# Softmax reciprocals of an attention kernel: two of 256 columns in place of four of 128

## The reference

```python
qkv = X @ W_qkv + b_qkv                     # 16 heads, 64 each for Q, K, V
scores = einsum('bhqd,bhkd->bhqk', Q, K) / sqrt(64)
attn = softmax(scores, axis=-1)             # over 1024 keys
out = einsum('bhqk,bhkv->bhqv', attn, V)
return out @ W_fc + b_fc
```

## Time and profile before

| | us |
|---|---|
| median of 3 runs | 1827.69 |
| lowest and highest | 1825.25, 1830.28 |
| the profiled execution | 1822.86 |
| its span in the trace | 1821.4 |
| busy in the span: TensorE | 1644.4 (90%) |
| VectorE | 1345.1 (74%) |
| POOL | 1130.2 (62%) |
| ScalarE | 829.1 (46%) |

### The profile page before, as it was taken

The page is one execution under the profiler, slowest core; times in us unless marked ns, Lnnn a source line. Parts: engine busy times, 40 slices in busy tenths (PEclk is TensorE's granted clock), DMA queues, the critical chain, the costliest instruction groups (busy, mean ns, idle before and its releaser), DMA issues. The chain is left out here.

```text
span 1821.4 us, 29000 instructions
## 1 busy us (share of the span) xinstructions
PE 1644.4 (90%) x9675; PEld 900.1 (49%) x9675; DVE 1345.1 (74%) x2143; ACT 829.1 (46%) x1144; POOL 1130.2 (62%) x519
## 2 busy tenths in 40 slices
PE   4789999999999999999999999999999999945996
PEld 3444444444444444444444444444445444434886
DVE  5678777777777777777777777777777777587887
ACT  3344444444444444444444444444444444325874
POOL 3366766776766667667676666766776766720134
PEclk8899999999999999999999999999999999968999
DMA  2000000000000000000000000000000001000010
GB/s 87 18 18 18 18 18 17 17 17 17 17 17 17 17 17 1 16 17 17 17 17 17 17 17 17 17 17 17 17 17 17 17 13 49 1 24 24 30 36 29
DMA packets 31040, 37.07 MB, mean 20 GB/s; under 512 B 2174, under 2 KB 25243, under 8 KB 31003
## 3 DMA queue, kind: packets, MB, share of 16 engines
q1 hardware_dynamic: 30848, 36.58, 6.2%
q10 hardware_dynamic: 154, 0.03, 0.0%
HBM read 14.58 MB, written 2.10 MB: 9 GB/s over the span
## 5 line engine op out<-in xcount | busy, mean ns | idle before, releaser
L511 POOL TENSOR_TENSOR ACC<-ACC,PR 128x1024 f32<-128x1024 f32 x382 | 908.4, 2378 | 345.4 <-ACT PR L548 325.8
L548 ACT ACTIVATE PR<-ps_s 128x1024 f32<-128x1024 f32 x512 | 501.1, 1024 | 525.9 <-PE ps_s L754 504.7
L586 DVE TENSOR_REDUCE NMH<-ps_mx 128x2 f32<-128x1024 f32 x507 | 617.6, 1218 | 151.7 <-PE ps_mx L734 148.4
L764 PE MATMUL ps_o<-PR,V 128*64 128x512 f32 x2048 | 507.6, 614 | 4.4 <-ACT PR L548 1.1
L734 PE MATMUL ps_mx<-KHI,QHI 64*128 64x512 f32 x1014 | 234.5, 457 | 60.0 <-DVE NMH L586 60.0
L622 DVE RECIPROCAL SUM<-SUM 128x128 f32<-128x128 f32 x256 | 240.4, 941 | 6.4 <-ACT SUM L539 6.4
L764 PEld LDWEIGHTS ps_o<-PR,V 128*64 128x64 f32 x2048 | 106.1, 135 | 272.4 <-ACT PR L548 252.6
L511 POOL TENSOR_TENSOR ACC<-PR 128x1024 f32<-128x1024 f32 x64 | 150.8, 2356 | 143.0 <-ACT PR L548 143.0
L748 PE MATMUL ps_s<-QHI,KHI 64*128 64x512 f32 x1024 | 210.6, 406 | 17.6 <-DVE QLO L600 16.3
L734 PEld LDWEIGHTS ps_mx<-KHI,QHI 64*128 64x128 f32 x1014 | 95.4, 184 | 255.3 <-DVE NMH L586 161.1
L750 PE MATMUL ps_s<-QLO,KHI 64*128 64x512 f32 x1024 | 203.9, 391 | 0.0
(11 more groups left out here) (192 smaller groups left out, 1722.2 us busy)
## 6 DMA issues: line engine op xcount, KB each, us to landing
hcur<-hT SPq DMA_DIRECT2D x32, 512.0 KB, 3.3
Wraw<-in_L_attn_W_qkv SPq DMA_DIRECT2D x32, 192.0 KB, 3.0
x<-in_L_attn_X SPq DMA_DIRECT2D x4, 512.0 KB, 5.2
Wfc<-in_L_attn_W_fc SPq DMA_DIRECT2D x32, 64.0 KB, 2.5
hT<-in_L_attn_X SPq DMA_DIRECT2D x4, 512.0 KB, 6.3
out<-e_res SPq DMA_DIRECT2D x7, 256.0 KB, 2.3
e_hTs<-hT_hi SPq DMA_DIRECT2D x6, 256.0 KB, 2.3
e_hTs<-hT_lo SPq DMA_DIRECT2D x6, 256.0 KB, 2.4
```

Of the source, the lines that this page charges most:

```text
L511: G.tensor_tensor(ACC[:, ch, :, :], a, PR[:, t, :, :], ALU.add).then_inc(added, 1)
L548: A.activation(PR[:, t, :, :], ps_s[:, i:i + 2, :], ACT.Exp, scale=SCALE).then_inc(exp_done, 1)
L586: D.tensor_reduce(NMH[:, ch, i, kc, :], banks, AX, ALU.max, negate=True).then_inc(mx_red, 1)
L764: last = T.matmul(ps_o[half(h), ch, :], V[:, u, t, half(h)], PR[:, t, h, :], start=(t == 0), stop=(t == 7))
```

## The change

The table INVERT loses its entries at (1,0), (2,0), (5,0) and (6,0); those at (1,1), (2,1), (5,1) and (6,1) now name parts 0 and 1. A part is 256 columns instead of 128, and O waits for two counts per chunk in place of four. In `last` two parts stand in place of four. Nothing else differs, and the result is computed from the same numbers.

```diff
--- before.py
+++ after.py
@@ -398,8 +398,8 @@
         SUMS = {0: (-1, 1), 4: (0, 0)}
         SUMS_BANK = 3
 
-        INVERT = {(1, 0): (-1, 1, 0), (1, 1): (-1, 1, 1), (2, 0): (-1, 1, 2), (2, 1): (-1, 1, 3), (3, 0): (-1, 1, "O"),
-                  (5, 0): (0, 0, 0), (5, 1): (0, 0, 1), (6, 0): (0, 0, 2), (6, 1): (0, 0, 3), (7, 0): (0, 0, "O")}
+        INVERT = {(1, 1): (-1, 1, 0), (2, 1): (-1, 1, 1), (3, 0): (-1, 1, "O"),
+                  (5, 1): (0, 0, 0), (6, 1): (0, 0, 1), (7, 0): (0, 0, "O")}
         LAST_ON_POOL = 6
         FIRST_UNITS = (("k", 0, ps_s[:, 0, :]), ("k", 1, ps_s[:, 1, :]), ("q", 0, ps_s[:, 2, :]), ("q", 1, ps_s[:, 3, :]),
                        ("v", 0, ps_o[:, 0, :]), ("v", 1, ps_o[:, 1, :]))
@@ -613,11 +613,11 @@
             def invert(m, ch, part):
 
                 if part == "O":
-                    dve.wait_ge(recip, 4 * (2 * m + ch + 1))
+                    dve.wait_ge(recip, 2 * (2 * m + ch + 1))
                     wait(dve, fc_mm, 2 * m + ch)
                     D.tensor_tensor(O[:, :], ps_o[:, ch, :], SUM[:, :], ALU.mult).then_inc(o_norm, 1)
                 else:
-                    q = slice(part * P, part * P + P)
+                    q = slice(part * 256, part * 256 + 256)
                     dve.wait_ge(sums_in, 2 * m + ch + 1)
                     D.reciprocal(SUM[:, q], SUM[:, q]).then_inc(recip, 1)
 
@@ -676,7 +676,7 @@
                     dve.wait_ge(added, 7 * (2 * NP - 1) + t - 1)
                     D.tensor_tensor(ACC[:, 1, :, :], ACC[:, 1, :, :], PR[:, t, :, :], ALU.add).then_inc(added, 1)
                 unit("fc", NP - 1, 1, 0, ps_s[:, 0, :])
-                for part in (0, 1, 2, 3, "O"):
+                for part in (0, 1, "O"):
                     invert(NP - 1, 1, part)
                 unit("fc", NP - 1, 1, 1, ps_s[:, 1, :])
```

## The result

The changed kernel takes 1836.1 us (median of 20 executions, 1828.6 to 1838.8) against 1828.4 us (20, 1825.3 to 1831.0) before: a ratio of 1.0038, 95% interval 1.0029 to 1.0047. It is slower by 7 us by the ratio (7.7 on the medians), a little beyond the 0.3% that a measurement of this kernel can tell. The profiled execution has a span of 1834.5 us against 1821.4. That is 13.1 us, more than the medians differ by, since the profiled execution of the kernel before took 1822.86 us, less than any of those 20.

The account below looks back on a forecast made before the run. TensorE was taken to set the pace, VectorE mattering only where TensorE waits for it. A 3.1 us stall less 0.06 at the end gave +3.0 us, 1830.7 us on the median's scale, range 1825 to 1839.5.

Parts of the forecast that it names:

- The wide reciprocal: A reciprocal of 256 columns on VectorE: 1.73 us, against 0.941 us for the narrow one of 128.
- Place (2,1): Behind block 2's second reduce: the wide reciprocal delays block 3's first reduce, stalling TensorE 0.10 us in 31 pairs, 3.1 us.
- Place (6,1): Behind block 6's second reduce: block 7's first reduce ends late, a 0.04 us stall that the V matmuls take back; cost 0.
- Places (1,1) and (5,1): Behind the second reduces of blocks 1 and 5, before the projections: 0.78 us more fits VectorE's 1.5 us idle; cost 0.
- The sum: Whole kernel: 3.1 us of stall in 31 pairs less 0.06 at the end, together +3.0 us.
- The range: Whole kernel: from 1825 us (all hidden, less the lowest run's 2.4 us) to 1839.5 us (a wide reciprocal of 1.88 us).
- the likeliest case: The small stall of TensorE before block 3's first reduce: 1830.7 us, +0.17%.
- the case to which I gave 0.30: Whole kernel slower by more than 0.3% (5.5 us), by any cause; chance 0.30.
- a wide one that saves nothing: Rival before block 3's first reduce: a wide reciprocal takes 1.88 us, total 1839.5 us; chance 0.30 with all other losses.
- What would show it: Signs in the profile: 1.73 us reciprocals, about 31 more maxima matmul waits, VectorE busy time down some 10 to 20 us.
- At the end: Behind the last chunk: two wide reciprocals take 3.33 us in place of 3.39 for four narrow ones, a gain of 0.06.

Follow-up runs that it names:

- p192_320: The changed kernel with its 512 columns cut into 192 and 320 in place of 256 and 256: 1859.6 us, 1.0161 against the kernel before.
- wide_ch0: The changed kernel with wide reciprocals only for chunk 0 and four narrow ones for chunk 1: 1828.5 us, 0.9997 against the kernel before.

## Why the prediction was right, and where it fell short

- *The wide reciprocal*: 1.73 us forecast, 1.742 measured.
- *Place (2,1)*: the reduce of (3,0) was to start 2.78 us behind that of (2,1) and does, at 2.80 (619.77 to 622.57). A stall of 0.16 less 0.06 from the V matmuls, so 0.10; the pair grew by 0.08, and the V matmuls went from 2.00 to 1.94 as forecast. The step holds, and p192_320 shows its slope.
- *Place (6,1)*: cost 0, as forecast (wide_ch0: 47.79 us). There the V matmuls took 1.96 us.
- *Places (1,1) and (5,1)*: "cost 0" holds in the regular pairs, where idle time of 0.7 us is left ahead of L600. It failed in the second pair. The step that failed is that I looked at one regular pair and took it for all: I named gate_rows in the description and never followed what stands behind the reciprocal there. Price 2.9 us, once.
- *The clock* was missing from the sum. By the profiles, stretches at 1.2 GHz in the loop cost 1.5 us each.
- *The sum*: +3.0 us forecast, +7.7 measured on the medians of the two kernels, +6.9 by the ratio. 2.4 stall and 2.9 waits make 5.3, so 1.6 to 2.4 us remain. The clock was my candidate for them, since the profiles of kernels with the stall at (2,1) have 3, 2, 1, 3, 1 and 4 stretches in the loop and those without it 0, 0, 1, 1 and 1. That is one execution each. The record has the mean granted clock of every execution, and by it the clock's part is smaller: 80 executions of the kernel before (those for which it stands) average 0.9725 and 1828.8 us, 25 of the changed one 0.9718 and 1835.4 us, and within either kernel 0.001 less clock goes with 0.9 to 1.1 us more. Of the 6.5 us between the averages the clock then makes 0.7, and 5.8 stay at an equal clock, near the 5.3 of the two waits. The three stretches against none, 4.5 us, are a difference between two single executions, of which the one before took 1822.86 us at a mean clock of 0.978. Nor is the part behind the attention still: with the same code it took from 220.2 to 229.1 us over these profiles.
- *The range* held the time (1825.0 to 1839.5), and the mechanism of the likeliest case acts near the size forecast (2.4 us for 3.1), but the change went over 0.3% and so into the case to which I gave 0.30. The range reached that far up for the price of a wide one that saves nothing. That rival did not act; the second pair took its place, and that the time stayed in the range is luck in that part.
- *What would show it*: I expected the new wait in the idle time of the maxima matmuls. It was in that of their weight loads, 161.1 to 178.6 us, 186 to 247 times. VectorE's busy time fell by 8.8 us, a little less than the 10 to 20 that I gave. At the end the reciprocals took 3.37 us in place of 3.39 (3.33 forecast).

## What to carry to other kernels

In an in-order queue that another engine waits on, the length of each single instruction counts, not the number: two long ones in place of four short ones save 8.8 us of busy time and cost 2.4 us where one stands in front of a reduce with 0.25 us of slack, and nothing where idle time of 1.5 us follows. Follow every unrolled pair of a loop, not the regular one alone. And before shaving a queue that is 74% busy, look at the one long wait for it: moving one instruction by one place there gave 62 us.

## What the runs showed of the hardware

- A reciprocal costs 6.2 ns a column and 0.15 us more, from 4 to 320 columns (171, 353, 941, 1343, 1742, 2141 ns for 4, 32, 128, 192, 256 and 320; each within 10 ns of that).
- The steps of gate_rows (512 columns on VectorE) last from 0.52 to 2.8 us, and those followed here by the point of POOL's add at which they start; the split of 256 columns lasts 0.43 us ahead of the adds and 2.2 us, at most 2.6, beside them. The reciprocals never do (1694 to 1753 ns over 128 of them).
- Each stretch at 1.2 GHz in a regular pair of 47.8 to 47.9 us (at 226, 994, 464, 652, 1179 and 1036 us, in five executions) began 1 to 2 us behind the start of the matmul that had waited 1.8 us in block 0. The one in the second pair of the changed kernel, at 158 us, began 0.4 us behind that of the matmul which had waited 1.90 us for QLO. With the wait of block 0 removed, the regular pairs of three traces had none, but neither had those of four traces with that wait.
